# A gated feed-forward kernel with a top-k mask on one core: block 3's x folded in place, and four orders moved

## The reference

```python
def attn_ref(x, w_gate, w_up, w_down):             # x (2,1024,1024), I = 2752
    s = silu(einsum('bsh,ih->bsi', x, w_gate))
    _, idx = top_k(-abs(s), I // 2)                # the smaller half of each token ...
    s = s with idx set to 0                        # ... is zeroed
    s = s * einsum('bsh,ih->bsi', x, w_up)
    return einsum('bsi,hi->bsh', s, w_down)

def qlora_linear(x, wq, A, B):                     # wq is a quarter as wide as the layer
    return x @ tile(wq, (1, 4)).T + (x @ A.T @ B.T) * 0.5      # rank 2

def ffn_ref(x, ...):
    return qlora_linear(silu(qlora_linear(x, w1q, a1, b1)) * qlora_linear(x, w3q, a3, b3), w2q, a2, b2)

x = layernorm(x + attn_ref(x, ...))
x = layernorm(x + ffn_ref(x, ...))
```

## Time and profile before

| | |
|---|---|
| median of 3 runs | 1878.03 us (1871.79 to 1878.9) |
| profiled execution | 1877.62 us; its span is 1875.8 us |
| PE busy | 1850.4 us of the span |
| DVE, ACT, POOL busy | 1454.0, 721.5, 954.6 us |

### The profile page before, as it was taken

How to read it: one execution, slowest core, us unless ns; L and a number is a source line. 1 busy time by engine, 2 the same in 40 slices (tenths; PEclk the granted TensorE clock), 3 DMA queues, 4 the chain that set the end, 5 groups by cost and what they waited for, 6 DMA issues and landing times. The chain is left out here.

```text
span 1875.8 us, 23805 instructions
## 1 busy us (share of the span) xinstructions
PE 1850.4 (99%) x8668; PEld 1543.2 (82%) x8668; DVE 1454.0 (78%) x2054; ACT 721.5 (38%) x1173; POOL 954.6 (51%) x705
## 2 busy tenths in 40 slices
PE   9999999999999999999999999999999999999998
PEld 8898878978889888888888988889887776887776
DVE  2138899788988695898869588988488999569973
ACT  4346534474233425622343365233333322213312
POOL 5456795445555764455576545555467332013410
PEclk9999999999999999999999999999999999999999
DMA  4333248624377733435685334376962111412212
GB/s 147 94 99 98 82 143 241 197 96 141 100 229 238 228 115 101 138 104 174 192 264 184 96 102 142 99 219 198 274 211 88 45 57 57 172 42 77 103 46 90
DMA packets 123224, 259.09 MB, mean 138 GB/s; under 512 B 13828, under 2 KB 35844, under 8 KB 119752
## 3 DMA queue, kind: packets, MB, share of 16 engines
q1 hardware_dynamic: 118496, 240.76, 41.0%
q10 hardware_dynamic: 4608, 16.78, 2.3%
HBM read 216.06 MB, written 41.42 MB: 137 GB/s over the span
## 5 line engine op out<-in xcount | busy, mean ns | idle before, releaser
L651 POOL TENSOR_TENSOR wl<-w_in_place,wh 128x512 fp32r<-128x512 f32 (+2 forms) x552 | 750.9, 1366 | 583.0 <-ACT wh L758 582.0
L758 ACT CAST wh<-w_in_place 128x512 fp32r<-128x512 f32 (+2 forms) x560 | 328.6, 589 | 720.7 <-DMA w_in_place<-in_wg 280.6
L1546 PE MATMUL banks<-wh,xTh 128*128 128x512 f32 (+2 forms) x1536 | 565.1, 368 | 6.6 <-POOL wl L651 6.6
L1547 PE MATMUL banks<-wl,xTh 128*128 128x512 f32 (+2 forms) x1536 | 563.2, 367 | 0.0
L1548 PE MATMUL banks<-wh,xTl 128*128 128x512 f32 (+2 forms) x1536 | 563.2, 367 | 0.0
L1546 PEld LDWEIGHTS banks<-wh,xTh 128*128 128x128 f32 x1536 | 288.4, 188 | 52.4 <-POOL wl L651 10.9
L1548 PEld LDWEIGHTS banks<-wh,xTl 128*128 128x128 f32 x1536 | 288.3, 188 | 40.2
L1547 PEld LDWEIGHTS banks<-wl,xTh 128*128 128x128 f32 x1536 | 288.4, 188 | 39.7
L1546 PE MATMUL banks<-wh,hTh 128*128 128x512 f32 x672 | 262.2, 390 | 5.5 <-POOL wl L651 5.4
L1547 PE MATMUL banks<-wl,hTh 128*128 128x512 f32 x672 | 261.6, 389 | 0.0
L1548 PE MATMUL banks<-wh,hTl 128*128 128x512 f32 x672 | 261.5, 389 | 0.0
(11 more groups left out here) (152 smaller groups left out, 2187.6 us busy)
## 6 DMA issues: line engine op xcount, KB each, us to landing
w_in_place<-in_wd SPq DMA_DIRECT2D x176, 256.0 KB, 2.7
w_in_place<-in_wg SPq DMA_DIRECT2D x128, 256.0 KB, 2.9
w_in_place<-in_wu SPq DMA_DIRECT2D x128, 256.0 KB, 2.7
turning<-squares SPq DMA_DIRECT2D x16, 1024.0 KB, 5.0
landed<-turning SPq DMA_DIRECT2D x64, 256.0 KB, 4.1
w_in_place<-in_w SPq DMA_DIRECT2D x54, 256.0 KB, 2.8
x_in_place<-in_xT SPq DMA_DIRECT2D x32, 256.0 KB, 5.1
y<-in_xtok SPq DMA_DIRECT2D x4, 2048.0 KB, 8.1
```

The costliest lines, as they stand in the source:

```text
L651: nc.gpsimd.tensor_tensor(lo, landed, hi.bitcast(F32), ALU.subtract).then_inc(done, 1)
L758: nc.scalar.copy(hi, piece).then_inc(hi_done, 1)
L1546: nc.tensor.matmul(dst, ah, bh, start=start, stop=False)
L1547: nc.tensor.matmul(dst, ah, bl, start=False, stop=False)
```

## The change

- **Block 3's x.** `turn_x`, `low_rank`, `turned_x`, `fold_x` and the tensor `a13s` go. DVE folds the normed tile where it lies in `y` (`late_folds`) into `xa`, and makes the rank-2 sums by tokens (`late_dots`), tiles 0 and 1 in second(0), tiles 2 and 3 in second(1). Its four factors (rows of `arow`) are loaded by `load_a_late`. At the end of down_2(1) PE does `turn_folded(3, k)`, twelve transposes, and ACT, DVE go on as for the other blocks (`high_xf`, `low_xf`, `low_rank_x`). ACT replicates the sums into `rep2`. Block 1's residual is now loaded over each tile of `y` when its sums are made (`load_y1`). ACT instead of DVE rounds the small part of `low_rank_h` (`high_t2`).
- **wd behind a search's first round.** The tuple is (1, 1, 2, 1, 1, 1) in place of (0, 2, 2, 1, 1, 1).
- **Norms between pieces of up.** ACT norms one tile after each of the first four pieces of chunk 2 and sends each two pieces later.
- **Twelve products of GpSimd.** The products of chunks 3, 4 and 5 of block 0 all stand behind the pieces 8 to 19 of gate(1); those of chunks 3 and 4 stood in chunks 4 and 5 of up(0), those of chunk 5 behind the pieces 8 to 11 of gate(1).

```diff
-XF_BANKS = ((4, 6, 5), (2, 3, 7), (5, 6, 7))
+XF_BANKS = ((4, 6, 5), (2, 3, 7), (5, 6, 7), (5, 6, 7))
+XA = (0, 1, 0, 0)
...
+            def load_a_late(c):
+
+                if c < 2:
+                    sp.wait_ge(acc_ready, 2)
+                elif c == 2:
+                    sp.wait_ge(b_ready, 2)
+                    sp.wait_ge(xf_out, 16 * NT * (NB - 1))
+                else:
+                    sp.wait_ge(xf_turned, 6)
                 sp.sem_inc(passed_sp, 1)
+                sp.dma_start(arows[c], arow[:, c, :]).then_inc(a_in, 16)
...
+            def load_y1(t):
+
+                sp.wait_ge(x1_out, 16 * NT * NB)
+                sp.wait_ge(tok_done, NT * (NB - 1) + t + 1)
+                sp.sem_inc(passed_sp, 1)
+                sp.dma_start(y[:, t, :], x1[1, :, t, :]).then_inc(y1_in[t], 16)
...
-                    if b == 1 and KH <= i < KH + NT:
-                        gate_times_up(NJ - 1, i - KH)
+                    if b == 1 and KH <= i < KH + 3 * NT:
+                        gate_times_up(NJ - 3 + (i - KH) // NT, (i - KH) % NT)
...
-                if j and 0 <= t < NT:
+                if 1 <= j < NJ - 2 and 0 <= t < NT:
                     gate_times_up(j - 1, t)
...
-                    if j == 1:
-                        norm(b - 1)
+                        if j == 2:
+                            norm(b - 1, i)
...
-                search(b, lambda: high_d(b - 1, next(ahead)), (0, 2, 2, 1, 1, 1))
+                search(b, lambda: high_d(b - 1, next(ahead)), (1, 1, 2, 1, 1, 1))
...
+            def late_folds(t):
+
                 if t == 0:
+                    dve.wait_ge(xf_turned, FOLDED.index((2, 2)) + 1)
+                dve.wait_ge(norm_done, NT * (NB - 1) + t + 1)
+                st.done()
+                step(V.tensor_tensor(halves[:, :], y[:, t, 0:H // 2], y[:, t, H // 2:H], ALU.add))
+                st.done()
+                step(V.tensor_tensor(xa[:, XA[3], t * HQ:(t + 1) * HQ], halves[:, 0:HQ], halves[:, HQ:2 * HQ], ALU.add))
+
+            def late_dots(t):
+
+                if t == 0:
+                    dve.wait_ge(a_in, 16 * 2 * R * NB)
+                for w in range(2):
+                    for r in range(R):
+                        st.done()
+                        ins = V.scalar_tensor_tensor(out=junkx[:, :], in0=y[:, t, :], scalar=1.0, in1=arows[R * w + r],
+                                                     op0=ALU.mult, op1=ALU.mult, accum_out=dots[:, 3, t, w, r:r + 1])
...
+                elif b == 1:
+                    take_out(1, 0)
+                    late_folds(2)
+                    late_dots(2)
+                    take_out(1, 1)
+                    late_folds(3)
+                    late_dots(3)
+                    sums(0)
+                    take_out(1, 2)
+                    sums(1)
+                    sums(2)
+                    for k in range(KQ):
+                        low_xf(3, k)
+                    low_rank_x(3)
+                    take_out(1, 3)
+                    sums(3)
+                    norm_bias(NB + 1)
...
-                    turn_next(t)
                     all_but_last(t, 1)
                     product(t, 1, CQ - 1)
-                    low_rank_next(t)
-
-            pe.wait_ge(small_in, 16 * 2)
+                if b == 1:
+                    for k in range(KQ + 1):
+                        turn_folded(3, k)
```

More of the change, by code:

```diff
@@ L390, in program @@
         y_in = [sem(f"y_in{i}") for i in range(2)]
+        y1_in = [sem(f"y1_in{t}") for t in range(NT)]
         passed_dve, passed_pool, passed_pe, passed_sp = (
@@ L624, in _ @@
                         load_xf(2)
+                        for c in (2, 3):
+                            load_a_late(c)
                     if h and p == PAIRS - 2:
@@ L987, in second @@
             def second(b):
+                if b != 1:
+                    high_t2(b)
                 if b == 0:
@@ L1514, in second, with sums @@
                     norm_bias(NB - 1)
-                for t in range(NT):
-                    if b == 1:
-                        fold_x(3, t)
-                    if b or t > 1:
-                        take_out(b, t)
-                    if b == 1 and t == NT - 1:
-                        low_rank_x(3)
+                    step(V.memset(rep2[:, :, :], 0.0))
+                    st.done()
+                    dve.sem_inc(rep_zero, 1)
+                def sums(t):
                     dve.wait_ge(e_evac, 2 * NT * b + 2 * (t + 1))
@@ L1524, in second @@
                     norm_sums(n, lambda t: y_tile(b, t), [t], slice(0, NT) if not last else FRONT if t < NT - 1 else BACK)
-                    if last and t == NT - 2:
-                        norm_bias(n, FRONT)
-                norm_bias(NB + b + last, BACK if last else slice(0, NT))
+                if b == 0:
+                    sums(0)
+                    sums(1)
+                    take_out(0, 2)
+                    sums(2)
+                    late_folds(0)
+                    late_dots(0)
+                    take_out(0, 3)
+                    sums(3)
+                    late_folds(1)
+                    norm_bias(NB)
+                    late_dots(1)
+                elif b == 1:
[5 more added lines that the diff above has]
+                    late_dots(3)
+                    sums(0)
+                    take_out(1, 2)
+                    sums(1)
+                    sums(2)
+                    for k in range(KQ):
+                        low_xf(3, k)
+                    low_rank_x(3)
+                    take_out(1, 3)
+                    sums(3)
+                    norm_bias(NB + 1)
+                else:
+                    for t in range(NT):
+                        take_out(b, t)
+                        sums(t)
+                        if last and t == NT - 2:
+                            norm_bias(NB + b, FRONT)
+                    norm_bias(NB + b + last, BACK if last else slice(0, NT))
             for b in range(2):
@@ L1794, in all_but_last @@
                         product(t, n, c)
-                def turn_next(t):
-                    if b == 0 and t == 0:
-                        for k in range(KQ + 1):
-                            turn_folded(2, k)
-                    if b == 1:
-                        turn_x(t)
-                def low_rank_next(t):
-                    if b == 1:
-                        low_rank(t)
                 bank_waits(0)
```

189 lines of the change are left out of this document (73 added, 116 removed).

## The result

The changed kernel takes 1863.61 us (median of 5 runs, 1859.32 to 1865.16) against 1877.94 for the kernel before on the same chip (5 runs, 1871.79 to 1878.90). The ratio is 0.9928, 95% interval 0.9915 to 0.9941. Forecast were 1864.0. The profiled execution after has a span of 1860.2 us, 15.6 less than the one before, at a mean granted clock of 0.998.

What follows compares the result with a forecast made beforehand. PE bounds the kernel, working 1850.4 of 1875.8 us. The terms -2.0 - 2.95 - 0.95 - 7.7 = -13.6 us on the profiled 1877.62 give 1864.0 us, range 1858 to 1871.

Steps and rivals of the forecast that it cites:

- Part 1: up(0) and gate(1): moving GpSimd's twelve products removes waits of PE on wl; -2.0 us.
- five waits: PE between 222 and 262 us, in up(0) and gate(1): all go, worth 4.3 us at most.
- Part 2: down(0 to 2): ACT rounds a wd piece in its idle before round two, so PE's waits go; -2.95 us.
- Part 3: Chunk 2 of up(1), up(2), up(3): norms spread over four pieces remove PE's idles; -0.95 us.
- Part 4: down_2(1): 10.5 us off PE's path, 1.3 of transposes added, a new wait of 1.5 behind them; -7.7 us.
- slack forecast: down_2(1): low_rank_h(1) ends at 1629.6, PE needs it at 1630.4; 0.8 us of slack.
- idle of 2.42 us before down_2(0): Second sub-layer's single large wait of PE, 2.4 us: the change leaves it as it is.
- give it all back: Rival, gate(1): disturbed rows hold to piece 19 and the start is later; Part 1 is 0, 1866.0 us; chance 0.10.
- strict rule on the shared port: Rival, gate(1): every product and wl waits for a DVE instruction; +5.9 us against today, 1871.9; chance 0.06.
- wait at take_out(1, 3): New wait of 1.5 us behind the transposes; rival: it passes 2.4 and the clock halves, 1866.6 us, chance 0.13.
- slow sums: Rival, Part 4: DVE's late sums take their usual 2.19 us, 0.96 more than undisturbed; 1880.3 us; chance 0.03.
- more goes than was counted: Rival: no wait at take_out(1, 3) and undisturbed products in gate(1); 1860.5 us; chance 0.10.

Runs made afterwards that it cites:

- e3: Changed kernel with the four norms put back in a row behind chunk 1 of up(1), up(2), up(3): 1861.59 us, ratio 0.9918.
- e1: Changed kernel with only the twelve products of GpSimd put back to where they stood: 1863.23 us, ratio 0.9932.
- e8: Changed kernel with each of the sixteen late sums by tokens made twice: 1884.53 us, ratio 1.0048 to the kernel before.
- e6: Changed kernel with DVE's two instructions on 102 x 2752 elements cut into four each by columns: 1863.51 us, ratio 0.9926.
- e5: Changed kernel with take_out(1, 3) put ahead of low_xf(3, k) and low_rank_x(3) on DVE: 1863.27 us, ratio 0.9919.

## Why the prediction was right, by its steps

- **Part 1** (-2.0; -2.05). The working came to 1.7 and took 2.0 for it. By the traces PE gains 3.4 us up to piece 8, loses 1.0 from there to piece 19 and 0.3 behind it; the two terms were each off (4.3 and 2.6 were counted) and made up for it. GpSimd ended the `wl` of piece 8 at 265.6 us, not 266.3, and took 32.7 us for the eleven pairs, not 32.4. The five waits of the earlier trace rows became two, 1.0 us in all. They lie at the start of gate(1), where POOL splits x and w in turn: these two I had counted as gone, and they stayed. One wait of 0.39 came at 278.91, as said, and its stretch ran at GpSimd's pace.
- **Part 2** (-2.95; -2.87). 1.75 us at the eighth piece of down(0) where 1.71 were counted; 0.8 and not 0.55 came back: 0.5 on the way to the fourth round's first piece at 410.19, where PE idled only 0.12, and 0.3 in the pieces behind it. In the other two searches 0.87 and 1.05 where 0.9 each were counted, with nothing given back, as said.
- **Part 3** (-0.95; -1.27). Right in kind, but above the bound of 1.1 that was given, and its sum takes 0.6 us for idles of 0.28, 0.28 and 0.15, which make 0.7: 0.52, 0.59 and 0.16 us in the three. The bound took the idles of one trace for the most that a lump of norms costs; e3 has them at 0.43, 1.02 and 0.19.
- **Part 4** (-7.7; -7.69). 9.38 us less in down_2(1) and 1.69 more behind the transposes. The sums took the undisturbed length, as the row below shows (count, ns least/median/most); one of sixteen was disturbed (2.20 us; the other four stand in a row of their own, at 1.22 to 1.23). low_rank_h(1) ended 0.4 us ahead of PE, half the slack forecast.

```profile
L1439 DVE SCALAR_TENSOR_TENSOR junkx<-y,arow x12: 1221/1224/2196, 1606.8 to 1638.0; 128x1024 int8<-128x1024 f32 x12
```

- **What failed.** Of the idle of 2.42 us before down_2(0) the prediction says that "the change leaves it as it is", and the stretches outside the four parts it counts at nothing: both were read from one execution as if they were fixed. The idle was absent in the profiled execution after (4.0 us less, with the clock behind it), the clock fell behind the idle at 1429.25 (1.6 us more), and gate(2) began 1.2 us worse. Other traces have each with the same code there and without it, so none is put down to the change. Only one run of each kernel's five was traced, so how such pieces fell in the others is not known. The parts' 13.9 us bear the forecast out; that 1864.0 met the median 1863.6 within 0.4 us, where runs of one kernel lie 6 to 7 us apart, is luck.
- **The rivals.** GpSimd did not give it all back (e1). The strict rule on the shared port did not hold for every instruction: of the twelve products four of 512 columns took 1.74 to 1.80 us, as it would have them, but of the four of 320 one took 0.86, and two `wl` in the same stretch 1.30. The wait at take_out(1, 3) stayed at 1.42 us and the clock at 1.00. The slow sums did not come; e8 bears out the chain from which their price was worked out. In the rival that more goes than was counted, 1.5 and 2.3 us off 1864.0 make 1860.2, not 1860.5.

## What to carry to other kernels

Work taken off the bounding engine is worth its full length only while the engine that takes it over stays ahead, so follow that engine's chain instruction by instruction and then look for the order inside it: here one reordered call gave back the 1.7 us that the new chain had cost. Before a gap in the trace is booked as fixed, ask whether it comes from two engines that fall in or out of step, and look at a second execution; stretches between the same two instructions can be compared where whole times cannot: down_2(1) takes 35.77 to 35.79 us in ten of the eleven traces with its new code (53.2 in e8, which forces it), while whole times of one kernel differ by 5. A stretch that itself varies, as gate(2)'s by 2.3 us, must be known as such first. Cutting a long instruction into pieces freed the engine that it blocked (e6), but the two then took turns, and whoever waited for the cut work waited longer.

## What the hardware did that was not expected

- In the thirteen traces PE's granted clock fell to its lower level, half of the full 2.4 GHz, for some of the time behind each of eight idles of 2.42 us and more (mean 0.50 to 0.76 over the next 2.8 us), and behind one of the 22 between 1.33 and 1.96 us (the idle of 1.6 us at each kernel's start left out). That one (after), and one of the eight (before), are below, as length, busy (instructions), clock, DMA share, GB/s; 1.80 us in e5 and 1.85 us in before left it at 1.00. In the four traces in which down_2(0) starts behind such an idle it takes 37.45 to 37.61 us to the start of down_2(1), where the others take 35.93 to 36.00: the lower clock costs 1.5 to 1.6 us there.

```profile
1429.25:1432.05 2.80, 2.80 (x7) 0.55 0.00 0
```
```profile
1580.98:1583.78 2.80, 2.80 (x7) 0.50 0.99 418
```

- DVE's copies of 128 x 16 elements took 1.33 us each beside GpSimd's stream of `wl` and 0.16 without, below; ACT does the same copy in 0.20. Each small copy on DVE thus took about as long as a whole `wl` of GpSimd (1.30 us).

```profile
L1398 DVE COPY rep<-dots x18: 163/1329/1349, 1406.5 to 1431.7; 128x16 f32<-128x16 f32 x18
```
```profile
L966 ACT COPY rep<-dots x12: 199/202/210, 1427.7 to 1636.1; 128x16 f32<-128x16 f32 x12
```

- In the stretch where the fifth load of w13 lands, the queue of instruction packets moves one packet of some 16 KB (68 packets, 1.11 MB in the whole trace after). In five of the seven traces with a late pair it starts 1.0 to 2.0 us behind the issue of the load's first half, in the other two 2.4 and 2.7 us behind it, and in the five with an early first half 2.3 to 2.6. Whether it delays the load, and which engine's code it carries, stays open.
